# A state-space scan kernel: the first product of each accumulator goes to ScalarE, the carried state enters through the first column of v, and the table of places is another one

## The reference, cut to what matters

```python
t = layernorm(groupnorm(x))                   # 8 x 1024 x 384
xm, z = split(t @ in_proj_w.T)                # 768 channels each
xc = silu(conv_over_positions(xm) + conv_b)
dt, Bm, Cm = split(xc @ x_proj_w.T, [24, 40])
dt = softplus(dt @ dt_proj_w.T + dt_proj_b)   # 1024 x 768
dA = exp(dt[:, d] * A[d, n])                  # 16 states n
dBu = dt * xc * Bm[:, n]
h = dA_t * h + dBu_t                          # one step per position, 1024 in a row
y[t, d] = sum over n of h[t, d, n] * C[t, n]
y = (y + xc * D) * silu(z)
x = x + mlp(y @ out_proj_w.T)
```

## Time and profile before

| | |
|---|---|
| median of 3 runs | 4217.63 us (4215.8 to 4219.98) |
| the profiled execution | 4216.37 us, its span 4214.7 us |
| busy over the span | PE 91%, DVE 83%, ACT 61%, POOL 61% |
| layer 0 | from the start to about 3414 us; the first scan starts at 92.03 us |
| layer 1 | the last 800 us, PE busy 785.7 of them |
| granted TensorE clock | 0.956 on average |

### The profile page before, as it was taken

How to read it: one execution, slowest core, us unless ns; L and a number is a source line. 1 busy time by engine, 2 the same in 40 slices (tenths; PEclk the granted TensorE clock), 3 DMA queues, 4 the chain that set the end, 5 groups by cost and what they waited for, 6 DMA issues and landing times. The chain is left out here.

```text
span 4214.7 us, 48609 instructions
## 1 busy us (share of the span) xinstructions
PE 3833.8 (91%) x15575; PEld 2297.3 (55%) x15575; DVE 3489.7 (83%) x4627; ACT 2589.2 (61%) x4102; POOL 2585.7 (61%) x1314
## 2 busy tenths in 40 slices
PE   6679898999898989989898989898979969999999
PEld 4344545454444545544544455444544458888887
DVE  5899999999999999999999999999999155555555
ACT  4667676767677776767676767677754234333433
POOL 3878787788878787878787878878775120000000
PEclk8779999999999999999999999999989979999999
DMA  5122222222222222222222222222222511111111
GB/s 180 41 70 65 91 67 84 79 79 74 87 64 87 86 78 91 66 90 66 88 67 85 76 85 72 88 63 88 76 70 82 198 45 56 40 40 40 40 40 35
DMA packets 147748, 317.90 MB, mean 75 GB/s; under 512 B 15388, under 2 KB 15772, under 8 KB 147012
## 3 DMA queue, kind: packets, MB, share of 16 engines
q1 hardware_dynamic: 139936, 281.74, 20.5%
q0 software_dynamic: 6832, 28.99, 1.9%
q10 hardware_dynamic: 756, 4.44, 0.3%
HBM read 289.36 MB, written 25.76 MB: 75 GB/s over the span
## 5 line engine op out<-in xcount | busy, mean ns | idle before, releaser
L575 POOL TENSOR_TENSOR vv<-big,bb 128x1536 f32<-128x1536 f32 x512 | 1768.2, 3455 | 594.0 <-DVE hh L615 580.0
L586 ACT ACTIVATE bank<-big,a_neg 128x512 f32<-128x512 f32 x1536 | 1045.1, 689 | 794.5 <-DVE hh L615 790.3
L675 PEld LDWEIGHTS bank<-ident,hh 128*128 128x128 f32 x6144 | 758.2, 146 | 1092.8 <-DVE yy L661 507.9
L675 PE MATMUL bank<-ident,hh 128*128 128x128 f32 x6144 | 1026.5, 288 | 257.9 <-DVE yy L661 161.7
L661 DVE SCALAR_TENSOR_TENSOR yy<-bank,ct,yy 128x384 f32<-128x384 f32 x1760 | 1032.5, 598 | 135.5 <-PE bank L675 131.6
L615 DVE TENSOR_TENSOR_SCAN hh<-bank,hl,vv 128x512 f32<-128x512 f32 x768 | 971.0, 1272 | 25.5 <-ACT bank L586 14.6
L615 DVE TENSOR_TENSOR_SCAN hh<-bank,vv 128x512 f32<-128x512 f32 x768 | 923.9, 1210 | 37.7 <-POOL vv L575 19.3
L795 PE MATMUL bank<-tt,wring 128*128 128x512 f32 x1152 | 556.2, 595 | 17.2 <-ACT tt L781 16.3
L826 PE MATMUL bank<-hid,wring 128*128 128x512 f32 x1152 | 552.8, 595 | 1.8 <-DVE xr L842 1.8
L1858 POOL DMA_DIRECT2D out<-xb x16 | 12.2, 765 | 804.8 <-DVE xb L1853 804.8
L1808 ACT ACTIVATE big<-bank,vv 128x512 f32<-128x512 f32 x192 | 132.2, 689 | 387.0 <-PE bank L1729 387.0
(11 more groups left out here) (174 smaller groups left out, 5016.1 us busy)
## 6 DMA issues: line engine op xcount, KB each, us to landing
bb<-b_rows SPq DMA_DIRECT2D x512, 256.0 KB, 3.3
wring<-in_w_m SPq DMA_DIRECT2D x192, 384.0 KB, 3.0
xb<-x_scratch SPq DMA_DIRECT2D x18, 768.0 KB, 4.5
xn<-in_x SPq DMA_DIRECT2D x16, 768.0 KB, 4.7
xr<-in_x SPq DMA_DIRECT2D x16, 768.0 KB, 6.2
x_scratch<-xr SPq DMA_DIRECT2D x16, 768.0 KB, 5.0
out<-xb POOLq DMA_DIRECT2D x16, 768.0 KB, 3.9
big<-in_x SPq DMA_DIRECT2D x14, 768.0 KB, 6.1
```

The costliest lines, as they stand in the source:

```text
L575: e_v.inc_by(eng.tensor_tensor(vv[:, k % 2, :, :], wu[:, G3 * g:G3 * g + G3, :], bb[:, k % NBB:k % NBB + 1, :].to_broadcast([P, G3, T]), A ...
L586: e_da.inc_by(eng.activation(da[t % NDA][:, :], dt[:, j, :], ACT.Exp, scale=a_neg[:, j, n:n + 1]))
L675: ins = eng.transpose(ht[c % NHT][:, i * P:(i + 1) * P], hh[:, k % 2, i, c * P:(c + 1) * P], ident[:, :])
```

## The change

Three things are done.

1. The products for n = 0 (L659, four chunks in slots 1 and 17) are made by ACT instead of DVE (`init_act`). `INITS` lists them; `MACS` lists what is left to DVE. ACT emits chunks 0 and 1 before the slot's first exp, chunks 2 and 3 before its second and third.
2. Scans of the second half start from 0.0 too. The carried state enters through v: since h_0 = dA_0*h_last + v_0, the first column of v gets dA_0*h_last added. POOL computes a*dt_0 for the 16 states and three tiles of a group (`carried_log`, 128x48), ACT takes exp of it (`carried_act`), POOL multiplies it into hl (`carried_state`), and after each v product of a second half POOL adds three values per partition to it (in `scan_pool`), waiting first for its own product. DVE waits for that add.
3. `ORDER`, `LAGS`, `BURST_QUOTA` (3 to 4) and `SPREAD_MASK` have other values. The mask had states 1, 6, 9, 11 and 13, and now has 1, 6, 11 and 13, so per unit two chunks (in slots 10 and 26) return from ACT and POOL to DVE.

```diff
-ORDER = ("Y3 Y4 Y5 pad:3:0:3 DT3 pad:5:0:10 DT4 GN0 pad:5:19:6 O0 O1 DT5 O2 MU0 M1.0 pad:1:0:0 "
...
+ORDER = ("Y3 Y4 pad:3:0:0 Y5 pad:5:0:14 DT3 GN0 pad:5:19:6 O0 DT4 O1 O2 DT5 MU0 M1.0 M1.1 "
...
-BURST_QUOTA = 3
-SPREAD_MASK = 10818
+BURST_QUOTA = 4
+SPREAD_MASK = 10306
...
-MACS = [(k, c) for k in range(SLOTS) for c in range(CH) if not spread(k, c)]
+INITS = [(k, c) for k in range(0, SLOTS, NS) for c in range(CH)]
+MACS = [(k, c) for k in range(SLOTS) for c in range(CH) if k % NS and not spread(k, c)]
...
@@ -572,9 +578,41 @@
                 e_w.wait(eng, u, G3 * g + G3 - 1)
             e_bb[k % NBB].wait(eng, u, k // NBB)
             scanned(eng, u, G3 * (k - 2) + G3 - 1)
-            e_v.inc_by(eng.tensor_tensor(
-                vv[:, k % 2, :, :], wu[:, G3 * g:G3 * g + G3, :],
-                bb[:, k % NBB:k % NBB + 1, :].to_broadcast([P, G3, T]), ALU.mult))
+            js = slice(G3 * g, G3 * g + G3)
+            product = eng.tensor_tensor(
+                vv[:, k % 2, :, :], wu[:, js, :],
+                bb[:, k % NBB:k % NBB + 1, :].to_broadcast([P, G3, T]), ALU.mult)
+            if not u.half:
+                e_v.inc_by(product)
+                return
+            e_vp.inc_by(product)
+            if k == 0:
+                carried_state(eng, u, 0)
+            eng.wait_ge(s_h0, u.b * NG + g + 1)
+            eng.wait_ge(e_vp.sem, u.b * SLOTS + k + 1)
+            first = vv[:, k % 2, :, 0]
+            e_v.inc_by(eng.tensor_tensor(first, first, hl[:, n, js], ALU.add))
+        def carried_log(eng, u, g):
+            js = slice(G3 * g, G3 * g + G3)
+            e_dt.wait(eng, u, G3 * g + G3 - 1)
+            eng.tensor_tensor(h0[:, :, :], a_neg[:, js, :],
+                              dt[:, js, 0:1].to_broadcast([P, G3, NS]), ALU.mult).then_inc(s_h0m, 1)
+        def carried_state(eng, u, g):
+            js = slice(G3 * g, G3 * g + G3)
+            eng.wait_ge(s_hl, u.b * SLOTS + NS * (g + 1))
+            eng.wait_ge(s_h0e, u.b * NG + g + 1)
+            part = hl[:, :, js]
+            eng.tensor_tensor(part, part, h0[:, :, :].rearrange("p j n -> p n j"),
+                              ALU.mult).then_inc(s_h0, 1)
+        def carried_act(eng, u, g):
+            eng.wait_ge(s_h0m, u.b * NG + g + 1)
+            eng.activation(h0[:, :, :], h0[:, :, :], ACT.Exp).then_inc(s_h0e, 1)
         def scan_act(eng, u, t):
             k, i = t // G3, t % G3
@@ -606,15 +644,14 @@
                     e_ht.wait(eng, u, CH * (k - 2) + CH - 1)
                 else:
                     e_ht.wait(eng, u, CH * (SLOTS - 2 + k) + CH - 1, back=1)
-                if u.half:
-                    wait_last(eng, u, SLOTS - 1 if k >= 2 else max(k, SLOTS - 2 + k))
-                elif k >= 2:
+                if u.half and k < 2:
+                    wait_last(eng, u, SLOTS - 2 + k)
+                elif not u.half and k >= 2:
                     wait_last(eng, u, k - 2)
             e_da.wait(eng, u, G3 * k + i)
-            start = hl[:, n, j:j + 1] if u.half else 0.0
             e_scan.inc_by(eng.tensor_tensor_scan(
                 hh[:, k % 2, i, :], da[(G3 * k + i) % NDA][:, :], vv[:, k % 2, i, :],
-                start, ALU.mult, ALU.add))
+                0.0, ALU.mult, ALU.add))
         def y_part(g, c):
             return yy[:, c, G3 * P * g:G3 * P * (g + 1)]
@@ -647,25 +684,33 @@
         def mac_dve(eng, u, k, c):
             g, n = scan_of(k)
-            if n == 0 and c == 0:
+            earlier = max(m for m in INITS + MACS if m < (k, c) and m[1] == c)
+            if earlier in INITS:
+                e_in.wait(eng, u, INITS.index(earlier))
+            else:
+                e_mac.wait(eng, u, MACS.index(earlier))
+            e_ht.wait(eng, u, CH * k + c)
+            y = y_part(g, c)
+            e_mac.inc_by(eng.scalar_tensor_tensor(
+                out=y, in0=ht[c % NHT][:, 0:G3 * P], scalar=ct[:, u.half, c, n:n + 1], in1=y,
+                op0=ALU.mult, op1=ALU.add))
+        def init_act(eng, u, k, c):
+            g, n = scan_of(k)
+            if c == 0:
                 e_cc.wait(eng, u)
                 e_yt.wait(eng, u, G3 * g + G3 - 1, back=1)
-            if n:
-                e_mac.wait(eng, u, MACS.index(max(m for m in MACS if m < (k, c) and m[1] == c)))
             e_ht.wait(eng, u, CH * k + c)
-            y = y_part(g, c)
-            scale = ct[:, u.half, c, n:n + 1]
-            if n == 0:
-                ins = eng.tensor_scalar(y, ht[c % NHT][:, 0:G3 * P], scale, None, ALU.mult)
-            else:
-                ins = eng.scalar_tensor_tensor(out=y, in0=ht[c % NHT][:, 0:G3 * P], scalar=scale,
-                                               in1=y, op0=ALU.mult, op1=ALU.add)
-            e_mac.inc_by(ins)
+            e_in.inc_by(eng.activation(y_part(g, c), ht[c % NHT][:, 0:G3 * P], ACT.Copy,
+                                       scale=ct[:, u.half, c, n:n + 1]))
         def scan_pe(eng, u, k, c):
             at = CH * k + c - NHT
             back, last = (0, (at // CH, at % CH)) if at >= 0 else (1, (SLOTS - 1, CH + at))
-            if spread(*last):
+            if last in INITS:
+                e_in.wait(eng, u, INITS.index(last), back=back)
+            elif spread(*last):
                 e_sc.wait(eng, u, SPREADS.index(last), back=back)
             else:
                 e_mac.wait(eng, u, MACS.index(last), back=back)
@@ -1431,16 +1476,29 @@
                     if k + 2 < SLOTS:
                         scan_sync(eng, scan, k + 2)
                 if name == "pool" and live:
+                    if scan.half and k == 0:
+                        carried_log(eng, scan, 0)
                     scan_pool(eng, scan, k)
+                    if scan.half and k == NS - 4:
+                        carried_log(eng, scan, 1)
+                    if scan.half and k == NS - 2:
+                        carried_state(eng, scan, 1)
                 if name == "pool" and scan and 0 <= k - SPREAD_LAG < SLOTS \
                         and spread(k - SPREAD_LAG, CH - 1):
                     spread_pool(eng, scan, k - SPREAD_LAG, CH - 1)
+                if name == "act" and live and scan.half and k == NS - 3:
+                    carried_act(eng, scan, 1)
                 if name == "act" and live:
                     for t in range(G3 * k + NDA if k else 0, G3 * (k + 1) + NDA):
+                        if (k - 1) % NS == 0 and t >= G3 * k + NDA:
+                            for c in ((0, 1), (2,), (3,))[t - G3 * k - NDA]:
+                                init_act(eng, scan, k - 1, c)
                         if t == G3 * (k + 1) + NDA - 1 and k >= 1 and spread(k - 1, CH - 1):
                             spread_act(eng, scan, k - 1, CH - 1)
                         if t < SLOTS * G3:
                             scan_act(eng, scan, t)
+                        if scan.half and t == NDA - 1:
+                            carried_act(eng, scan, 0)
                     if not scan.half:
                         last_act(eng, scan, k)
                 if name == "pe":
@@ -1464,7 +1522,7 @@
                         for i in range(G3):
                             scan_dve(eng, scan, k, i)
                             for c in macs_after(i, k in bursts):
-                                if k >= 1 and not spread(k - 1, c):
+                                if k >= 1 and (k - 1, c) in MACS:
                                     mac_dve(eng, scan, k - 1, c)
                             dense_dve(BURST_QUOTA if k in bursts and i == 1 else DVE_QUOTA)
                         if k == SLOTS - 1:
```

More of the change, by code:

```diff
@@ L479, in layer0 @@
         e_da, e_v, e_scan = ev("dA", SLOTS * G3), ev("v", SLOTS), ev("scanned", SLOTS * G3)
+        e_vp = ev("v_product", SLOTS)
+        s_h0m, s_h0e, s_h0 = sem("h0_log"), sem("h0_decay"), sem("h0")
         e_ht, e_mac, s_hl = ev("hT", SLOTS * CH), ev("mac", len(MACS)), sem("h_last")
+        e_in = ev("y_begun", len(INITS))
         e_sc, e_ad = ev("scaled", len(SPREADS)), ev("added", len(ADDS))
```

7 lines of the change are left out of this document (4 added, 3 removed), and 19 rows, old and new, of tables (LAGS, ORDER).

## The result

The changed kernel takes 4208.71 us (median of 20 runs, 4206.43 to 4211.02), the one before 4216.83 (20 runs, 4215.12 to 4222.06): ratio 0.9981, 95% interval 0.9974 to 0.9987. That is 8 us faster where 58 were forecast, and outside the range. The profiled execution of the changed kernel took 4206.99 us, its span 4205.3, at a mean granted clock of 0.949.

What follows compares the result with a forecast made beforehand. DVE, the engine with the most work, was taken as the bound. First halves gain 2.5 us, second 4.8, a pair 7.3, eight pairs 59: from 4216.4 to 4157, with 1.3 for the median 4159; range 4118 to 4200.

Steps and rivals of the forecast that it cites:

- Slot 1: Four products for n = 0 leave DVE in slot 1; all 2.06 us come back in both halves.
- Slot 17: Four products leave DVE, but its scan waits 1.5 us for ACT's exp; 1.0 and 0.8 of 2.06 us come back.
- Scans of the second half: Scans without carried start value take 6.0 us less on DVE; 4.4 come back, bounds 3.0 and 6.0.
- The start of a second half: At the unit's start the 128x48 pieces and the add on POOL delay the scan: 0.9 us lost.
- The adds of 128x3: 32 carried-state adds on POOL per second half make v 0.32 us later each, mostly hidden; 1.0 lost at crowded slots.
- The third rival: POOL becomes the bound of the second half and the kernel is slower: 4265 us, chance 0.06.
- the port rule of the Trainium skill: VectorE and GpSimd share an SBUF port, so POOL's 32 adds would take back up to 6.1 us from DVE.
- Two chunks back on DVE: Chunks in slots 10 and 26 cost DVE 1.02 us per unit; less POOL and ACT work gives 0.5 back.
- The table of places: New places for dense work and dt pairs cost nothing, bounds 1.5 us per unit either way.
- the new places fit worse: Rival: new places lose 1.5 us in each unit and 2.0 in slots 17 to 20: 4215 us, chance 0.05.
- Other engines take it over: Rival: only slot 1 returns; POOL's adds use up the scans' gain, ACT slot 17's: 4201 us, chance 0.15.
- the two ends cancel: First and last unit lack a neighbour's work; the last has less for PE and POOL, the first more waiting: no net effect.

Runs made afterwards that it cites:

- the old places: The changed kernel with ORDER, LAGS, BURST_QUOTA and SPREAD_MASK of the kernel before (one lag differs): 4186.04 us, ratio 0.9929 to the kernel before.
- old_places_slot1: The changed kernel with the table of before, and the products for n = 0 on ACT in slot 1 alone, slot 17's on DVE again: 4183.71 us.
- the light pair: The kernel before and the changed kernel, both with every second inner product of PE's dense stages left out: 4131.62 and 4098.03 us.
- old_places_new_mask: The changed kernel with ORDER, LAGS and BURST_QUOTA of before but the new SPREAD_MASK: 4195.48 us, ratio 0.9951 to the kernel before.

## Why the prediction was wrong, step by step

- **Slot 1: right.** 2.06 forecast, 2.0 and 2.1 measured, in both halves. Nothing was late there.
- **Slot 17: the step that failed most.** "PE has time left in most slots" was read from one pair of starts and applied to all; in unit 8 of the kernel before, PE has no wait over 0.15 us in 21 of slots 0 to 30. "Of these DVE is busy 188.64" was read as the bound of each slot. In slots 17 and 18 both are full, and when DVE is relieved PE still needs all of the 11.5 us. The exp's wait of 1.5 came as forecast, but the 1.0 and 0.8 that I gave back on top of it were measured, with the old places, as a loss of 0.4 and 0.6. That is 2.8 us per pair, or 22 us. `old_places_slot1` confirms that nothing is to be had there. PE is not the only cause: in the light pair 0.7 of the 1.8 came back, so about 1.1 of the 2.8 stay with ACT's order even when PE has room. The prediction took the price of the dense work per product and never summed it by slot.
- **Scans of the second half: mis-sized.** 4.4 less 1.0 for crowded slots was forecast, 1.8 measured: 0.2 in each slot led by DVE, none in others. The difference between the halves (3.0) was taken as the least that could come back and was no bound: with the start values alike, second halves fell by 1.8 only. What the other 1.2 are stays open. 13 us.
- **The start of a second half: 1.4 instead of 0.9.** POOL's steps were counted; the small exp stands behind two large ones and a table load on ACT (put ahead of the two, it gave 0.6 of them back). 4 us.
- **The adds of 128x3: right in their price.** 0.20 us, start 0.14 after the record of their product ends, hidden in nearly all slots. DVE's waits for POOL in four units rose from 8.2 to 12.2 (forecast 12), but that this sum fits is partly luck: in the two second halves the starts rose by 2.8 (1.8 forecast) and slot 15 by 2.0 (2.0 forecast); in the first halves the starts rose by 0.9 and the crowded slots fell by 1.7. The wait in slot 15 cost no time: slots 14 to 16 take as long as before, so the 1.0 per second half that the sum put there came to nothing. The third rival did not come about; nor did the port rule of the Trainium skill ("Perfetto Trace Analysis", section "Optimizing Scalar/DVE Operations"): the scans' mean is 1.214 us beside POOL with 256 instructions more, against 1.210 for the scans from 0.0 before.
- **Two chunks back on DVE: the cost right, the return too small.** 0.5 each in slots 10 and 26 as worked out; where I gave back 0.5 per unit, the slots right behind gave back 1.5 in a first half and 1.2 in a second (`old_places_new_mask`). But for slot 3 the chunks cost nothing, and bring 0.5 and 0.1.
- **The table of places: costed at nothing, bounds of 1.5 per unit.** With the mask it took 0.7 and 2.6 us in the two halves, 3.3 per pair where 1.0 was forecast for the mask: 18 us. Its 22.7 us are 1.4 per unit, inside the bounds. 8 of the 22.7 are slot 3 at the lower clock in five units (5 x 1.66); the rest is order, as +0.6 in slots 3 and 4 of first halves, whose slot 3 is at the higher clock, and +0.4 and +0.3 in slots 12 and 13.
- **The clock: not considered.** The profile before gave 0.956 as a mean, and I didn't ask where the rest lies. Slots 31 to 2 hold it, right ahead of slot 3 with its out_proj products.
- Of the rivals, "the new places fit worse" (4215) came nearest in number, and its 1.5 per unit is what the table costs (1.4); but the 2.0 more that it laid on slots 17 to 20 are not the table's (0.1 or less there). "Other engines take it over" (4201) named the other part, with PE beside ACT and hardly with POOL. Neither alone is what happened.

The terms for the pair, with the old places: forecast 8.4 us (4.1 slot 1, 1.8 slot 17, 3.4 scans less POOL, less 0.9 start), measured 3.5 (4.1, less 1.0, 1.8, less 1.4). Then the table takes 3.3 of these 3.5. Eight pairs explain the 58 that were forecast and are gone; the 8 that are there come mostly from the last unit. The prediction let the two ends cancel, which they did not.

What isn't shown: which of the table's entries cost the rest; the mask was tried apart, single pads and lags were not. Slots 17 and 18 with ACT out of the way and PE as before were not run either. Nor is it shown why the clock falls in slot 3 in one unit and not in the next.

## What to carry to other kernels

Where several in-order queues pace each other slot by slot, sum each engine's need per slot, and count relief only where the relieved engine leads, and only down to what the next engine needs there; the busy time of a unit does not tell who leads a slot. Before work is taken off one engine and a hand-written table is changed with it, measure the two apart: here the table hid three quarters of what the edit gave. When a stretch gets shorter, look at what the granted clock does in the stretch behind it.
